# Expert stage: weight slots and token halves placed at other remainders of 128 bytes

## The chip, the cores and the metric

One core of a Trainium2 chip runs the whole program in one launch. The metric is the device time of that core in microseconds (us); lower is better. TensorE is called PE below and its weight loads PEld; DVE is VectorE, ACT ScalarE, POOL GpSimd, SP SyncE.

## The reference

The input is 8 sequences of 512 tokens with 256 features. Four blocks of retention and a small feed-forward part (with group and layer norms) come first, then a mixture of 8 experts, on which the change lies:

```python
x = layernorm(x + attn(x, ...))                 # 4 layers
gates = entmax_bisect(x @ Wr + br)              # 8 experts
h = relu(einsum('td,edf->etf', x, W1) + b1)     # 256 -> 1024
y = einsum('etf,efd->etd', h, W2) + b2          # 1024 -> 256
out = layernorm(x + einsum('td,te->td', y, gates))
```

All is float32 at inputs and outputs.

## The kernel before

**Precision.** A float32 product is made of three matmuls. `mm3` (L1569 to L1571) multiplies the high half of the stationary operand by the high and by the low half of the moving operand, then the stationary low half by the moving high half. A "half" here is the part of a value that one fp32r operand carries (high), or what is left (low); `both` and the pairs of lists hand them in. So every product of the expert stage is three matmuls of 128x512, each with a weight load of its own.

**Work of the expert stage.** The sequences are taken in 4 pairs. In each pair the stage runs over 32 quads (an expert and a block of 256 of its hidden features), 128 quads in all. A quad has 7 products from tokens to hidden (`product`) and 8 products from hidden to output (`down`). That is 21 and 24 matmuls, 45 in a quad and 5,760 in all. Seven and not eight products are needed because a Strassen-like scheme works with sums of weight blocks and sums of token blocks.

**Operands of a quad.** The stationary operands are columns of a weight slot `m_w`: 11 blocks of 128 columns, high halves first (`we_hi`), then the low halves (`we_lo`). There are four slots (`RING`), and quad q uses slot q % 4. The moving operands of `product` are `te_hi` and `te_lo`, the token halves, in two copies: copy 0 for pairs 0 and 2 ("even pairs"), copy 1 for pairs 1 and 3. The moving operands of `down` are `hid_hi` and `hid_lo`.

**Who fills the slots.** In pair 0 POOL forms the sums of weights, ACT writes the high halves (L883) and DVE the low halves (L1251), and SP stores each finished slot to DRAM as `prepared`. In pairs 1 to 3 SP loads the slot back: `load_prepared(q)` waits until quad q - 4 has been used up, and is issued three quads ahead of its own.

**Order of the work.** It is written out by hand. For each quad w, PE runs the products of quad w + 1 between the downs of quad w, so that ACT, DVE and POOL have time for bias, relu and the split of the hidden values. All engines are held together by semaphores with fixed counts.

**Memory.** Everything large lies in one arena of SBUF. `line_up` puts its base at a remainder of 64 when divided by 128, and `place(name, shape, at)` puts a tensor at base + `at` in each partition. All offsets `at` of the expert operands, and all steps inside them, are multiples of 128 bytes, so before the change every slot and every token half starts at remainder 64. One pair of tensors of the earlier layers is different: `h_sp`, the moving operand of the retention product, has rows of 258 floats (1032 bytes). Its four row blocks b = 0, 1, 2, 3 therefore start at remainders 64, 72, 80 and 88.

Of the kernel before, what the change touches and what calls it, by code (L numbers as in the profile page):

```python
# [20 lines left out]
F32R = mybir.dt.float32r  # L21
# [4 lines left out]
P = 128  # L26
# [22 lines left out]
def network(nc, x, Wkqv, Wm1, bm1, Wm2, bm2, gn_g, gn_b, Wf1, bf1, Wf2, bf2, ln_g, ln_b,  # L49
# [7 lines left out]
    B, S, D = x.shape  # L57
# [6 lines left out]
    A_, B_ = 0, 1  # L64
# [23 lines left out]
    SPLIT = 11 * P  # L88
# [13 lines left out]
    with ExitStack() as ctx:  # L102
# [52 lines left out]
        KB = 1024  # L155
        HEAD, TAIL_A = 60 * KB + 256, 14 * KB
        RAW, FOLDED, PLAIN = 0, 16 * KB, 28 * KB
        WORK = [48 * KB + s * (HEAD + TAIL_A) for s in range(SLOTS)]
        LAST = [at + HEAD for at in WORK]
        ENDING = LAST[B_] + TAIL_A  # L160
# [4 lines left out]
        def place(name, shape, at, dt=F32):  # L165
            return nc.alloc_sbuf_tensor_at(name, shape, dt, offset=base + at)
# [14 lines left out]
        def halves(name, s, shape, at):  # L181
# [16 lines left out]
        xs, hs = (place(f"m_{n}s", [P, 2, TB, D], RAW + i * 8 * KB) for i, n in enumerate("xh"))  # L198
        margin = hs[:, 0, 0:2, :].rearrange("p k d -> p (k d)").rearrange("p (n a b) -> p n a b", n=NB, a=E)
        slots = [place(f"m_w{n}", [P, 2, SPLIT], at, F32R)  # L200
                 for n, at in enumerate((WORK[A_] + 8 * KB, FOLDED, PLAIN, LAST[A_]))]
        we_raw = place("we_raw", [P, RAWS, 12 * P], WORK[B_])
        acc = [place(f"m_acc{n}", [P, DC, 2 * S], at) for n, at in enumerate((WORK[A_], WORK[B_] + 50 * KB + 256))]
        t_sum = place("t_sum", [P, 4, S], WORK[A_] + 19 * KB)
        te_hi = [place(f"te_hi{n}", [P, 7, S], at, F32R) for n, at in enumerate((WORK[A_] + 27 * KB, WORK[B_] + 36 * KB + 256))]
        te_lo = [place(f"te_lo{n}", [P, 7, S], at, F32R) for n, at in enumerate((WORK[A_] + 41 * KB, LAST[B_]))]
        sum1, sum2 = (place(f"sum{n + 1}", [P, S], WORK[A_] + (55 + 2 * n) * KB) for n in range(2))
        hid_hi = place("hid_hi", [P, 4, S], WORK[B_] + 12 * KB + 256, F32R)
        full = place("full", [P, 4, S], WORK[B_] + 20 * KB + 256)
        hid_lo = place("hid_lo", [P, 4, S], WORK[B_] + 28 * KB + 256, F32R)  # L210
        out_scaled = place("out_scaled", [P, 4, S], PLAIN + 11 * KB)
        gate_bc = [[place(f"gate_bc{n}{t}", [P, S], at) for t, at in enumerate(places)]
                   for n, places in enumerate(((ENDING, ENDING + 2 * KB), (WORK[B_] + 58 * KB + 256, LAST[A_] + 11 * KB)))]

        bias_rows = place("bias_rows", [E * 2 * FP + E * DC, P], ENDING)

# [1696 lines left out]
def build(nc, x, Wkqv, Wm1, bm1, Wm2, bm2, gn_g, gn_b, Wf1, bf1, Wf2, bf2, ln_g, ln_b,  # L1913
          Wr, br, W1, b1, W2, b2, score_floor, out):
    B, S, D = x.shape
    L = Wkqv.shape[0]
    pairs = B // 2
    h_store = nc.dram_tensor("h_store", ((L + 1) * pairs, 2, S, D), F32, kind="Internal").ap()
    folded = nc.dram_tensor("folded", (L, P, 6 * D), F32, kind="Internal").ap()
    quads = Wr.shape[1] * W1.shape[2] // (2 * P)  # L1920
    prepared = nc.dram_tensor("prepared", (quads, P, 22 * P), F32, kind="Internal").ap()
    gate_rows = nc.dram_tensor("gate_rows", (pairs, Wr.shape[1] * 2 * S), F32, kind="Internal").ap()
    network(nc, x, Wkqv, Wm1, bm1, Wm2, bm2, gn_g, gn_b, Wf1, bf1, Wf2, bf2, ln_g, ln_b,
            Wr, br, W1, b1, W2, b2, score_floor, out, h_store, folded, gate_rows, prepared)
# [23 lines left out]
```

## Time and profile before

| what | us |
|---|---|
| median of 3 runs | 2564.38 (2563.68 to 2564.65) |
| the profiled execution, its own time | 2561.24 |
| span of the profile, first to last instruction | 2559.5 |
| PE busy | 2448.3 |
| DVE busy | 1547.1 |
| ACT busy | 1370.8 |
| POOL busy | 1356.6 |
| mean granted TensorE clock, share of full | 0.987 |

The profile is of one execution. A matmul's busy time overlaps the next one's, since matmuls are pipelined; what a matmul costs is the distance from its start to the next start. The expert stage's first product starts at 1140.7 us and its last down product ends near 2542 us.

### The profile page before, as it was taken

The page shows a single profiled execution, that of the slowest core. Times are in us where ns is not written, and L with a number is a line of the kernel's source. Part 1 is how long each engine was busy: PE and PEld are TensorE (multiplying, and loading weights), DVE is VectorE, ACT ScalarE, POOL GpSimd, SP SyncE. Part 2 cuts the span into 40 slices and gives each one's busy share as a digit, 9 for nine tenths or more (in the row PEclk, how much of TensorE's full clock was granted, in tenths as well). Part 3 has the DMA queues.
Part 4 walks back from the last instruction along what each step waited for, and adds up shares of the span by engine and source line. Part 5 has one row for each costly group of instructions (what it writes and reads, how often), then busy time and mean ns, then how long its engine had stood idle before and what let it go on. Part 6 is the DMA issues. An engine that isn't in the chain of part 4 may idle for free. (4 is left out here: it accounts for less than half of the span.)

```text
span 2559.5 us, 35493 instructions
## 1 busy us (share of the span) xinstructions
PE 2448.3 (96%) x11766; PEld 2033.9 (79%) x11766; DVE 1547.1 (60%) x2976; ACT 1370.8 (54%) x2412; POOL 1356.6 (53%) x1256
## 2 busy tenths in 40 slices
PE   7999999999999999987999999999999999999997
PEld 5788878887888788876878778878888788888886
DVE  1566666656666666677777765656546566455545
ACT  4566666666666666654545554444444444444443
POOL 2244554445444654565777965546555456555454
PEclk9999999999999999998999999999999999999999
DMA  5110111001211112013655564543445344444441
GB/s 161 62 34 33 33 31 62 26 22 33 74 33 33 34 42 67 25 64 134 216 189 179 190 216 169 179 150 144 153 161 186 143 150 147 152 155 171 153 152 70
DMA packets 104582, 283.45 MB, mean 111 GB/s; under 512 B 7024, under 2 KB 77056, under 8 KB 88064
## 3 DMA queue, kind: packets, MB, share of 16 engines
q1 hardware_dynamic: 104320, 281.75, 32.0%
q8 instruction: 69, 1.13, 0.2%
q14 instruction: 65, 0.53, 0.1%
q10 hardware_dynamic: 128, 0.03, 0.0%
HBM read 212.16 MB, written 69.60 MB: 110 GB/s over the span
## 5 line engine op out<-in xcount | busy, mean ns | idle before, releaser
L658 POOL TENSOR_TENSOR hid_lo<-full,hid_hi 128x512 fp32r<-128x512 f32 x384 | 498.6, 1313 | 569.5 <-ACT full L931 460.1
L1365 DVE SCALAR_TENSOR_TENSOR full<-ps,bias_cols,sum 128x512 f32<-128x512 f32 x384 | 288.0, 750 | 207.7 <-PE ps L1571 193.9
L1569 PE MATMUL ps<-hid_hi,m_w 128*128 128x512 f32 x1024 | 403.8, 394 | 0.0
L1570 PE MATMUL ps<-hid_lo,m_w 128*128 128x512 f32 x1024 | 400.7, 391 | 0.0
L1571 PE MATMUL ps<-hid_hi,m_w 128*128 128x512 f32 x1024 | 400.5, 391 | 0.0
L1569 PE MATMUL ps<-te_hi,m_w 128*128 128x512 f32 x896 | 354.5, 396 | 21.0 <-DVE full L1365 14.2
L928 ACT ACTIVATE hid_hi<-ps,bias_cols 128x512 fp32r<-128x512 f32 x128 | 88.3, 690 | 495.9 <-PE ps L1571 495.9
L1570 PE MATMUL ps<-te_lo,m_w 128*128 128x512 f32 x896 | 351.2, 392 | 0.0
L1571 PE MATMUL ps<-te_hi,m_w 128*128 128x512 f32 x896 | 351.0, 392 | 0.0
L935 ACT ACTIVATE hid_hi<-full 128x512 fp32r<-128x512 f32 x256 | 161.7, 631 | 167.3 <-DVE full L1365 167.2
L590 POOL TENSOR_TENSOR pf_sp<-tmp,pf_sp 128x512 fp32r<-128x512 f32 x128 | 163.8, 1317 | 164.8 <-ACT pf_sp L852 164.8
L1569 PEld LDWEIGHTS ps<-hid_hi,m_w 128*128 128x128 f32 x1024 | 193.8, 189 | 40.7 <-issue 0.2
L1571 PEld LDWEIGHTS ps<-hid_hi,m_w 128*128 128x128 f32 x1024 | 193.5, 189 | 40.9
L1570 PEld LDWEIGHTS ps<-hid_lo,m_w 128*128 128x128 f32 x1024 | 193.8, 189 | 38.9
L1569 PEld LDWEIGHTS ps<-te_hi,m_w 128*128 128x128 f32 x896 | 169.5, 189 | 66.9 <-DVE full L1365 19.4
L1352 DVE TENSOR_TENSOR sum<-ps,sum 128x512 f32<-128x512 f32 x128 | 88.4, 691 | 202.5 <-PE ps L1571 181.9
L1571 PEld LDWEIGHTS ps<-te_hi,m_w 128*128 128x128 f32 x896 | 169.7, 189 | 36.1
L1570 PEld LDWEIGHTS ps<-te_lo,m_w 128*128 128x128 f32 x896 | 169.6, 189 | 34.4
L606 POOL TENSOR_SCALAR_AFFINE_SELECT pf_sp<-pf_sp 128x128 fp32r<-128x128 f32 x256 | 65.0, 293 | 196.3 <-DVE pf_sp L1096 196.3
L671 POOL TENSOR_TENSOR m_acc<-m_acc,out_scaled 128x512 f32<-128x512 f32 x124 | 166.7, 1344 | 0.0
L1356 DVE TENSOR_TENSOR sum<-ps,sum 128x512 f32<-128x512 f32 x128 | 88.1, 688 | 119.7 <-PE ps L1571 119.6
L936 ACT ACTIVATE full<-full 128x512 f32<-128x512 f32 x256 | 159.1, 622 | 0.0
(199 smaller groups left out, 5692.9 us busy)
## 6 DMA issues: line engine op xcount, KB each, us to landing
m_w<-prepared SPq DMA_DIRECT2D x96, 1408.0 KB, 6.0
prepared<-m_w SPq DMA_DIRECT2D x32, 1408.0 KB, 5.8
h_store<-h_out SPq DMA_DIRECT2D x32, 512.0 KB, 3.2
we_raw<-in_L_ffn_W SPq DMA_DIRECT2D x64, 256.0 KB, 6.4
gate_bc<-gate_rows SPq DMA_DIRECT2D x64, 256.0 KB, 6.3
h_in<-h_store SPq DMA_DIRECT2D x24, 512.0 KB, 4.3
h_in<-in_L_attn_x SPq DMA_DIRECT2D x8, 512.0 KB, 5.1
raw<-in_L_attn_Wf SPq DMA_DIRECT2D x8, 512.0 KB, 7.9
```

Source lines behind the costliest of these rows:

```text
L590: nc.gpsimd.tensor_tensor(out=lo, in0=full, in1=f32(hi), op=ALU.subtract).then_inc(done, n)
L658: nc.gpsimd.tensor_tensor(out=hid_lo[:, k, :], in0=full[:, k, :], in1=f32(hid_hi[:, k, :]), op=ALU.subtract).then_inc(hid_ready, 1)
L671: nc.gpsimd.tensor_tensor(out=at, in0=at, in1=out_scaled[:, j, :], op=ALU.add).then_inc(acc_added, 1)
L928: nc.scalar.activation(hid_hi[:, k, :], src, ACT.Relu, bias=bias)
L935: nc.scalar.activation(hid_hi[:, k, :], src, ACT.Relu)
L936: nc.scalar.activation(full[:, k, :], src, ACT.Relu).then_inc(relu_ready, 1)
L1352: nc.vector.tensor_tensor(out=sum2[:, :], in0=bank_b, in1=sum1[:, :], op=ALU.add).then_inc(sums, 1)
L1356: nc.vector.tensor_tensor(out=sum3[:, :], in0=bank_b, in1=sum1[:, :], op=ALU.add).then_inc(sums, 1)
L1365: nc.vector.scalar_tensor_tensor(out=full[:, k, :], in0=src, scalar=b1_col(e, 2 * fp + BLOCK_ROW[k]), in1=other[:, :], op0=ALU.add, op1=AL ...
L1569: nc.tensor.matmul(out, w[0], x[0], start=first, stop=False, skip_group_check=True)
L1570: nc.tensor.matmul(out, w[0], x[1], start=False, stop=False, skip_group_check=True)
L1571: return nc.tensor.matmul(out, w[1], x[0], start=False, stop=last, skip_group_check=True)
```

## The change

It moves tensors in the arena and nothing else. Weight slot 0 stays at remainder 64; slot 1 goes 32 bytes up to 96; slot 2 goes 16 bytes up to 80 (it is written as a view that leaves out the first 4 floats of a tensor that is 4 floats longer); slot 3 goes 96 bytes up to 32. Both token halves of even pairs go 160 bytes up to 96. The halves of odd pairs, and `hid_hi` and `hid_lo`, stay at 64. What lies next to a moved tensor (`t_sum`, `sum1`, `sum2`, `out_scaled` and one `gate_bc`) is pushed up by 128 or 256 bytes, which keeps its remainder.

```diff
         slots = [place(f"m_w{n}", [P, 2, SPLIT], at, F32R)
-                 for n, at in enumerate((WORK[A_] + 8 * KB, FOLDED, PLAIN, LAST[A_]))]
+                 for n, at in enumerate((WORK[A_] + 8 * KB, FOLDED + 32, PLAIN, LAST[A_] + 96))]
+        slots[2] = place("m_w2_shifted", [P, 2 * SPLIT + 4], PLAIN, F32R)[:, 4:].rearrange("p (n c) -> p n c", n=2)
-        t_sum = place("t_sum", [P, 4, S], WORK[A_] + 19 * KB)
-        te_hi = [place(f"te_hi{n}", [P, 7, S], at, F32R) for n, at in enumerate((WORK[A_] + 27 * KB, WORK[B_] + 36 * KB + 256))]
-        te_lo = [place(f"te_lo{n}", [P, 7, S], at, F32R) for n, at in enumerate((WORK[A_] + 41 * KB, LAST[B_]))]
-        sum1, sum2 = (place(f"sum{n + 1}", [P, S], WORK[A_] + (55 + 2 * n) * KB) for n in range(2))
+        t_sum = place("t_sum", [P, 4, S], WORK[A_] + 19 * KB + 128)
+        te_hi = [place(f"te_hi{n}", [P, 7, S], at, F32R) for n, at in enumerate((WORK[A_] + 27 * KB + 160, WORK[B_] + 36 * KB + 256))]
+        te_lo = [place(f"te_lo{n}", [P, 7, S], at, F32R) for n, at in enumerate((WORK[A_] + 41 * KB + 160, LAST[B_]))]
+        sum1, sum2 = (place(f"sum{n + 1}", [P, S], WORK[A_] + (55 + 2 * n) * KB + 256) for n in range(2))
-        out_scaled = place("out_scaled", [P, 4, S], PLAIN + 11 * KB)
+        out_scaled = place("out_scaled", [P, 4, S], PLAIN + 11 * KB + 128)
-                   for n, places in enumerate(((ENDING, ENDING + 2 * KB), (WORK[B_] + 58 * KB + 256, LAST[A_] + 11 * KB)))]
+                   for n, places in enumerate(((ENDING, ENDING + 2 * KB), (WORK[B_] + 58 * KB + 256, LAST[A_] + 11 * KB + 128)))]
```

No engine gets an instruction more or less, and none stands at another place in its order.

## Rows read from the trace of the kernel before

**Rows 1.** The page: span, and busy us (share) xinstructions of each engine

```profile
span 2559.5 us, 35493 instructions
PE 2448.3 (96%) x11766; PEld 2033.9 (79%) x11766; DVE 1547.1 (60%) x2976; ACT 1370.8 (54%) x2412; POOL 1356.6 (53%) x1256
```

**Rows 2.** Busy us by stretch, pairs 1 to 3; columns in the first line

```profile
core 0: us, PE busy (x) PEld busy (x) DVE busy (x) ACT busy (x) POOL busy (x), PEclk, DMA share, GB/s
1526.60:1867.30 340.70, 336.83 (x1506) 277.84 (x1505) 198.74 (x308) 153.43 (x273) 180.78 (x141) 0.99 0.44 158
1867.30:2208.00 340.70, 336.86 (x1506) 277.77 (x1505) 198.72 (x308) 153.41 (x273) 180.74 (x141) 0.99 0.45 158
2208.00:2544.00 336.00, 335.10 (x1486) 276.47 (x1485) 171.70 (x257) 149.03 (x262) 168.65 (x133) 1.00 0.41 145
```

**Rows 3.** Waits of PE: who waited, for whom, total us, times, longest us

```profile
PE ps L1569 <- DVE ry_sp L1096: 19.9, 21, 4.3
PE ps L1569 <- DVE full L1365: 14.2, 9, 3.3
```

**Rows 4.** PE's timeline, pair 2: start us, length us, engine, line, operation

```profile
1899.95 0.39 PE L1569 MATMUL ps<-hid_hi,m_w 128*128 128x512 f32 x1
1900.17 0.39 PE L1570 MATMUL ps<-hid_lo,m_w 128*128 128x512 f32 x1
1900.40 0.39 PE L1571 MATMUL ps<-hid_hi,m_w 128*128 128x512 f32 x1
1900.63 0.39 PE L1569 MATMUL ps<-te_hi,m_w 128*128 128x512 f32 x1
...
1901.31 0.39 PE L1569 MATMUL ps<-hid_hi,m_w 128*128 128x512 f32 x1
```

**Rows 5.** Groups by form, weight loads: busy us, mean ns | idle before

```profile
L1570 PEld LDWEIGHTS ps<-hid_lo,m_w 128*128 128x128 f32 x1024 | 193.8, 189 | 38.9
L1570 PEld LDWEIGHTS ps<-te_lo,m_w 128*128 128x128 f32 x896 | 169.6, 189 | 34.4
```

**Rows 6.** PE's timeline, one retention product: its last four row blocks

```profile
393.25 0.28 PE L1569 MATMUL ps<-h_sp,pf_sp 128*128 128x258 f32 x1
...
393.61 0.28 PE L1569 MATMUL ps<-h_sp,pf_sp 128*128 128x258 f32 x1
...
393.97 0.28 PE L1569 MATMUL ps<-h_sp,pf_sp 128*128 128x258 f32 x1
...
394.33 0.28 PE L1569 MATMUL ps<-h_sp,pf_sp 128*128 128x258 f32 x1
394.45 0.28 PE L1570 MATMUL ps<-h_sp,pf_sp 128*128 128x258 f32 x1
394.57 0.28 PE L1571 MATMUL ps<-h_sp,pf_sp 128*128 128x258 f32 x1
```

**Rows 7.** Groups by form, POOL and ACT: splits of 128x1024, and slots written

```profile
L590 POOL TENSOR_TENSOR h_sp<-h_in,h_sp 128x1024 fp32r<-128x1024 f32 x32 | 75.5, 2358 | 52.0 <-ACT h_sp L809 52.0
L590 POOL TENSOR_TENSOR w_plain<-raw,w_plain 128x1024 fp32r<-128x1024 f32 x8 | 19.1, 2390 | 0.0
L809 ACT ACTIVATE h_sp<-h_in 128x1024 fp32r<-128x1024 f32 x32 | 33.6, 1051 | 0.0
L790 ACT ACTIVATE w_plain<-raw 128x1024 fp32r<-128x1024 f32 x8 | 8.3, 1051 | 4.0 <-PE ps L1571 4.0
L1251 DVE TENSOR_TENSOR m_w<-we_raw,m_w 128x1408 fp32r<-128x1408 f32 x32 | 65.5, 2046 | 0.0
```

**Rows 8.** DMA issues: xcount, KB each, median us from issue to landing

```profile
m_w<-prepared SPq DMA_DIRECT2D x96, 1408.0 KB, 6.0
prepared<-m_w SPq DMA_DIRECT2D x32, 1408.0 KB, 5.8
```

**Rows 9.** Timelines: SP issues quad 72's load; PE starts its first product

```profile
1930.13 0.32 SPq L457 DMA_DIRECT2D m_w<-prepared  x1
...
1950.83 0.39 PE L1569 MATMUL ps<-te_hi,m_w 128*128 128x512 f32 x1
```

## The prediction

> **What bounds the kernel now.** I read the page first. PE is busy for 96% of the span, no other engine for more than 60% [rows 1]. Then the expert stage by stretches, because the change lies there alone. A pair takes 340.70 us and PE is busy for 336.8 of it, DVE for 199, POOL for 181, ACT for 153 [rows 2]. Then PE's waits: over the whole program the longest group that lies in the expert stage is 14.2 us behind DVE's L1365 [rows 3]. So PE sets the end, and nothing counts that does not change the distance between its matmuls, or make it wait.
>
> The timeline gives that distance. Six matmuls start between 1899.95 and 1901.31, so a matmul of 512 columns costs 1.36 / 6 = 0.227 us, the same with hidden values as with tokens [rows 4]. At the full clock of 2.4 GHz 512 columns are 213 ns; about 13 ns are left over in each. A quad of 45 matmuls is 45 x 0.2267 = 10.2 us, and 32 quads are 326.4 of the 340.7 us of a pair. The weight load of a matmul has 189 ns on its own track, less than 227 [rows 5]: it runs beside the matmul before.
>
> **The change, part by part.** The order of all engines stays, so every term is a duration that could change.
>
> *1. Matmuls with an operand that moved.* Slots 1 to 3 serve 3/4 of the 5,760 matmuls, 4,320. Slot 0 with the tokens of even pairs adds 64 / 4 = 16 quads x 21 = 336. Together 4,656 matmuls read something at a new remainder. The trace of before has no stationary operand that starts anywhere but at 64, and nothing that starts at 96 or 32. The nearest rows are those of `h_sp`, the moving operand whose row blocks start at 64, 72, 80 and 88. The four triples of one product start at 393.25, 393.61, 393.97 and 394.33, so the triples at 64, 72 and 80 take 0.36 us each; at 88 the first two matmuls take 0.24, as do two thirds of 0.36 [rows 6]. The rows have steps of 0.01 us, so a triple could hide 0.01 us, 3.3 ns in a matmul. The bounds are thus 0 and 3.3 ns x 4,656 = +15.4 us. A gain of the same size can't be excluded by these rows either: -15.4 us. I take 0.3 ns, near nothing, because 72, 80 and 88 read like 64: +1.4 us.
>
> *2. Weight loads.* The same loads begin at 96, 80 and 32. Each may take 227 - 189 = 38 ns more, a fifth of its length, before its track is full [rows 4, 5]. The cover is the matmul before it. If it were gone, each ns over these 38 would cost 4,320 ns, 4.3 us. The nearest row for a start off the usual remainder is again that of rows 6, with no price seen. I take 0.
>
> *3. ACT, DVE and POOL on the moved tensors.* In pair 0 ACT and DVE write 32 slots, 24 of them moved; ACT and POOL write the token halves of even pairs. Rows 7 compare a split of 1,024 elements into `h_sp` (three of four row blocks off remainder 64) with one of 1,024 into `w_plain` at 64: POOL 2358 against 2390 ns, ACT 1051 against 1051. No price, or a gain of 1%. DVE has no such pair; the bounds by POOL's rows are -1% and +1% of 24 x 2046 ns, -0.5 and +0.5 us [rows 7], and it is covered: PE's waits behind DVE in this stage come from L1365 and sum to 14.2 us [rows 3]. I take 0.
>
> *4. DMAs.* A load of a slot lands 6.0 us after its issue, and a store 5.8 [rows 8]. Quad 72's load is issued at 1930.13 and its first product starts at 1950.83, 20.7 us later [rows 9]; so 14.7 us are spare. Loads come once in a quad, about 10.65 us (340.7 / 32) apart [rows 2]. The cost of a misaligned start is bounded by 0 (no row of another remainder) and by the landing itself doubled, +6 us. Even doubled it lands 8.7 us early and before the next is issued (12.0 against 10.65 only just overlaps). The cover is the ring of four slots. Cost 0. In pair 0 a store twice as slow would delay `high_weights`, four quads (over 40 us) later: 0 too.
>
> *5. Neighbours.* They move by whole multiples of 128 bytes: 0.
>
> Sum: +1.4 us on the profiled execution's own 2561.24, hence 2562.6 there. The median of the runs, 2564.38, is 3.1 us above that execution; with the same +1.4 it becomes **2565.8 us**.
>
> Here is a rule against rows: 13 ns above 512 columns stand in each matmul [rows 4]. The Trainium skill (TensorE: Matmul & The Clock Gate, back-to-back measurements in Part 1) gives N / 2.4 + 2.5 ns, 215.7 for 512 columns, so by it 11 ns of ours come from something else. Its Part 2 says that PE has two independent read ports, one for the stream and one for weight loads; by that the 11 ns are no collision of the two reads, and placing them apart returns nothing.
>
> **The rivals.** A difference of 0.2%, 5.1 us, is about what a measurement of this kernel can tell from none.
>
> *Rival A, slower: a stream that starts off a 64-byte boundary takes one piece more.* 2,048 bytes at remainder 64 or 0 are 32 pieces of 64 bytes; at 96 they are 33. A matmul's stream would grow by 1/32 of 213 ns, 6.7 ns. It hits the tokens of even pairs, 64 quads x 21 = 1,344 matmuls: +9 us, **2573 us**. It decides from 3.8 ns on (5.1 us / 1,344). For it: no row shows a start at 96. Against it: `h_sp` at 72, 80 and 88 also starts off such a boundary and takes 0.36 us like 64 [rows 6], though 258 columns there are 16.1 pieces, and 17 are touched either way. That exception makes the row weak, so the rival keeps weight. If the weight loads pay as well, one piece on 8 is 189 / 8 = 24 ns, under the 38 ns of cover. Were the cover not real (PE swaps its weights only after the load has drained), then 4,320 loads would bring up to 24 ns x 4,320 = 104 us.
>
> The Trainium skill (SBUF — State Buffer, Door 1) says that SBUF has lines of 16 bytes, and that each access which crosses to a new line pays. All new remainders are multiples of 16; by it the number of lines stays at 128 for a stream, and rival A does not exist.
>
> *Rival B, faster: the 13 ns are the load's and the stream's reads meeting, and unlike remainders part them.* After the change moving and stationary remainders differ in 4,320 matmuls (all but slot 0 in downs, 768, slot 0 in odd pairs, 336, slot 1 in even pairs, 336). All 13 ns gone: -56 us, **2508 us**. For it: the 13 ns have no cause in the trace. Against it: in rows 6 the stationary `pf_sp` lies at 64 and `h_sp` at 64, then 72, then 80; unlike remainders take the same 0.36.
>
> *Rival C, much slower: the same meeting, but made worse.* Another 13 ns on 4,320 matmuls: +56 us, **2620 us**. Against it the same rows.
>
> *Rival D, nothing at all,* by granted clock alone: clock 0.99 against 1.00 in rows 2 is up to 3.4 us for a pair. This is inside the forecast's own range.
>
> **How the numbers follow.** No change beyond 0.2% (the forecast and D): 0.60. Rival A with its streams alone, 0.19, or with part of the weight loads' cost, 0.08: slower. Rival C 0.04. An unnamed small price that passes 5.1 us (1.1 ns x 4,656, inside the bound of term 1) 0.03. That gives slower 0.34. Rival B, whole or in part, 0.06: faster. The forecast's own range is 2561 (a pair's clock a little better, -3.4) to 2569.5. The range reaches on to A with its full bound: 2564.4 + 15.4 = 2580, and a little of A with weight loads, to 2588. It leaves out B and C and most of the weight-load case, under 2 in 10 together. Low end 2561.
>
> **What would show it.** Right: in the changed kernel six matmuls take 1.36 us in every slot and in both kinds of pair; a pair stays at 340.7 us; weight loads stay at 189 ns; loads of slots land at about 6 us. Slot 2 has a name of its own and so rows of its own; if they differ from the other slots', the 16 bytes matter. Rival A: pairs 0 and 2 grow by 4.5 us each while pair 1 stays. If weight loads pay, pairs 1 and 2 both grow, and the distance follows the slot with a period of four quads. Rival B or C: slot 0 keeps 0.227 us in odd pairs, and the others go to 0.214 or 0.240. I am wrong if any pair's length moves by more than 3 us.

## The result, and the profile after

| | before | changed |
|---|---|---|
| median us | 2564.52 (2563.68 to 2565.03, 4 runs) | 2587.53 (2581.75 to 2591.84, 4 runs) |
| the profiled execution, its own time | 2561.24 | 2581.75 |
| its span | 2559.5 | 2580.0 |

The changed kernel is slower: 1.009 of the time before, 95% interval 1.0078 to 1.0103, 23 us by the medians. The page shows where: PE alone.

```profile
span 2580.0 us, 35493 instructions
PE 2470.9 (96%) x11766; PEld 2030.4 (79%) x11766; DVE 1551.7 (60%) x2976; ACT 1370.8 (53%) x2412; POOL 1355.6 (53%) x1256
```

Against [rows 1] PE is busy 22.6 us longer with as many matmuls; ACT has what it had, POOL 1.0 us less, and DVE 4.6 us more, of which 2.9 us are one group, the split of hidden values (853 ns each before, 876 now). PE does not wait longer for DVE: the 14.2 us of [rows 3] read 12.9 now. The stretches of pairs 1 to 3 answer to [rows 2]. Each is cut where its first token product starts; pair 3 ends with PE's last transposes, about 5 us behind its last down product:

```profile
1524.50:1873.40 348.90, 345.35 (x1507) 279.12 (x1506) 199.33 (x308) 153.48 (x273) 180.17 (x140) 0.99 0.44 154
1873.40:2220.80 347.40, 343.65 (x1507) 277.77 (x1506) 199.52 (x308) 153.41 (x273) 180.31 (x140) 1.00 0.44 155
2220.80:2567.90 347.10, 344.57 (x1497) 278.06 (x1495) 176.09 (x264) 148.95 (x262) 167.88 (x132) 1.00 0.39 140
```

Pairs 1 and 2 took 340.70 us each in [rows 2]. Pair 3, cut the same way in the kernel before:

```profile
2208.00:2547.30 339.30, 336.71 (x1497) 277.66 (x1495) 174.93 (x264) 149.03 (x262) 168.65 (x133) 1.00 0.40 144
```

So the pairs grow by 8.2, 6.7 and 7.8 us, each with all of it in PE's busy time. 7.8 us on 32 x 45 = 1,440 matmuls is 5.4 ns in each. Pair 0 goes only from 385.9 to 387.8 us. PE is idle for some 29 us of it in both kernels, and its granted clock was 0.97 in this execution against 0.96, which gives back up to 3.9 us (0.01 x 386). Averaged over all matmuls of pair 0 that follow one another at the full clock, the distance went from 227.4 to 231.7 ns, 6.2 us on 1,440. The clock records have 27.9 us of the pair at 1.2 GHz before and 21.3 in the changed kernel; half of the difference, 3.3 us, came back. That leaves 2.9 us, and 1.9 were measured:

```profile
1136.70:1524.50 387.80, 358.88 (x1526) 284.42 (x1525) 280.57 (x379) 197.87 (x315) 280.69 (x238) 0.97 0.55 186
```

```profile
1140.70:1526.60 385.90, 356.43 (x1525) 287.34 (x1524) 278.83 (x379) 197.86 (x315) 279.94 (x238) 0.96 0.55 187
```

The first of these two rows is of the changed kernel, the second of the kernel before. The four pairs make 24.6 us. The earlier layers, which the change does not touch, ended 4.0 us sooner in this execution, which leaves the 20.5 us by which the spans differ. Most of the 4.0 is the granted clock: the clock records ahead of the stage have 20.5 us at 1.2 GHz before and 13.7 here, and half of the difference is 3.4 us. This execution is also the fastest of the four of the changed kernel, so the 20.5 us are less than the 23 of the medians.

PE's timeline in pair 2, where [rows 4] had 1.36 us for six matmuls:

```profile
1958.53 0.40 PE L1570 MATMUL ps<-te_hi,m_w 128*128 128x512 f32 x1
1958.77 0.40 PE L1571 MATMUL ps<-te_lo,m_w 128*128 128x512 f32 x1
1959.01 0.39 PE L1572 MATMUL ps<-te_hi,m_w 128*128 128x512 f32 x1
1959.24 0.39 PE L1570 MATMUL ps<-hid_hi,m_w 128*128 128x512 f32 x1
1959.47 0.39 PE L1571 MATMUL ps<-hid_lo,m_w 128*128 128x512 f32 x1
1959.70 0.39 PE L1572 MATMUL ps<-hid_hi,m_w 128*128 128x512 f32 x1
1959.93 0.39 PE L1570 MATMUL ps<-te_hi,m_w 128*128 128x512 f32 x1
```

Six matmuls now take 1.40 us, 233 ns each, and the distances are uneven: 0.24, 0.24, 0.23, 0.23, 0.23, 0.23. No wait stands between them. The rest stayed. Loads of a slot land as in [rows 8], also for slot 2, which is 16 bytes off and has a name of its own; DVE writes that slot in 1952 ns and the others in 2067, [rows 7] had 2046:

```profile
m_w<-prepared SPq DMA_DIRECT2D x72, 1408.0 KB, 6.0
...
m_w_shifted<-prepared SPq DMA_DIRECT2D x24, 1408.0 KB, 6.0
```

```profile
L1252 DVE TENSOR_TENSOR m_w<-we_raw,m_w 128x1408 fp32r<-128x1408 f32 x24 | 49.6, 2067 | 0.0
L1252 DVE TENSOR_TENSOR m_w_shifted<-we_raw,m_w_shifted 128x1408 fp32r<-128x1408 f32 x8 | 15.6, 1952 | 0.0
```

### The profile page after: what moved, and what is told of

Read it like the earlier page. It is cut to its first block and busy times, and to the rows that moved or that the text cites. A ratio compares the mean times of both kernels' runs of the same rounds, so it can differ in the third digit from the quotient of the medians.

```text
span 2580.0 us, 35493 instructions
## 1 busy us (share of the span) xinstructions
PE 2470.9 (96%) x11766; PEld 2030.4 (79%) x11766; DVE 1551.7 (60%) x2976; ACT 1370.8 (53%) x2412; POOL 1355.6 (53%) x1256
## 5 line engine op out<-in xcount | busy, mean ns | idle before, releaser
L1570 PE MATMUL ps<-hid_hi,m_w 128*128 128x512 f32 x768 | 305.1, 397 | 0.0
L1571 PE MATMUL ps<-hid_lo,m_w 128*128 128x512 f32 x768 | 304.9, 397 | 0.0
L1572 PE MATMUL ps<-hid_hi,m_w 128*128 128x512 f32 x768 | 303.0, 395 | 0.0
L1570 PE MATMUL ps<-te_hi,m_w 128*128 128x512 f32 x672 | 268.7, 400 | 18.5 <-DVE full L1366 12.6
L1571 PE MATMUL ps<-te_lo,m_w 128*128 128x512 f32 x672 | 265.8, 396 | 0.0
L1572 PE MATMUL ps<-te_hi,m_w 128*128 128x512 f32 x672 | 265.3, 395 | 0.0
L1570 PEld LDWEIGHTS ps<-hid_hi,m_w 128*128 128x128 f32 x768 | 145.2, 189 | 34.5 <-issue 0.3
L1570 PEld LDWEIGHTS ps<-te_hi,m_w 128*128 128x128 f32 x672 | 127.1, 189 | 57.5 <-DVE full L1366 17.1
L1572 PEld LDWEIGHTS ps<-hid_hi,m_w 128*128 128x128 f32 x768 | 145.1, 189 | 33.5
L1571 PEld LDWEIGHTS ps<-hid_lo,m_w 128*128 128x128 f32 x768 | 145.1, 189 | 32.6
L1572 PEld LDWEIGHTS ps<-te_hi,m_w 128*128 128x128 f32 x672 | 126.8, 189 | 29.9
L1571 PEld LDWEIGHTS ps<-te_lo,m_w 128*128 128x128 f32 x672 | 126.9, 189 | 27.9
```

The costliest lines, as they stand in the source:

```text
L1570: nc.tensor.matmul(out, w[0], x[0], start=first, stop=False, skip_group_check=True)
L1571: nc.tensor.matmul(out, w[0], x[1], start=False, stop=False, skip_group_check=True)
L1572: return nc.tensor.matmul(out, w[1], x[0], start=False, stop=last, skip_group_check=True)
```

## The experiments

Three theories stood at the start. "Off 64": an operand that starts at another remainder than 64 costs something by itself. "Unlike": a stream and the weight load that runs beside it cost something when their remainders differ. "Mixing": what costs is that remainders change from one matmul to the next.

In all that follows pair 3 is the meter. Its granted clock reads 1.00 in every kernel, while pairs 1 and 2 hold from 3.4 to 13.7 us at half clock, which differs from run to run (an average of 0.98 in place of 0.99 is 3.4 us of length). Before, pair 3 took 339.3 us. All the kernels with moved slots or tokens keep the change's pushed neighbours (`t_sum`, `sum1`, `sum2`, `out_scaled`, `gate_bc`), except `arena_96`.

### tokens_only: tokens of even pairs at 96, slots back at 64

```diff
-        te_hi = [place(f"te_hi{n}", [P, 7, S], at, F32R) for n, at in enumerate((WORK[A_] + 27 * KB, WORK[B_] + 36 * KB + 256))]
-        te_lo = [place(f"te_lo{n}", [P, 7, S], at, F32R) for n, at in enumerate((WORK[A_] + 41 * KB, LAST[B_]))]
+        te_hi = [place(f"te_hi{n}", [P, 7, S], at, F32R) for n, at in enumerate((WORK[A_] + 27 * KB + 160, WORK[B_] + 36 * KB + 256))]
+        te_lo = [place(f"te_lo{n}", [P, 7, S], at, F32R) for n, at in enumerate((WORK[A_] + 41 * KB + 160, LAST[B_]))]
```

> Only the token halves of even pairs stand at 96; all weight slots are back at 64. In the changed kernel pairs 1 to 3 each grew by about 8 us (340.7 to 348.9 and 347.4), 5.6 ns in a matmul. Theory 'unlike' (a stream and a weight load that run together at different remainders cost some 5 ns): only the 21 token matmuls of a quad pay, so pair 2 grows by 21/45 of 8 = 3.7 us, pairs 1 and 3 by nothing, in all about +5 us. Theory 'off 64' (only what itself starts off remainder 64 pays): the same, +5 us at most. Theory 'mixing' (remainders that change from matmul to matmul break a steady cadence, whatever they are): pair 2 grows by the full 8 us, hidden-value matmuls at 64 included, pairs 1 and 3 by nothing: about +10 us.

Measured: 2572.86 us against 2564.88, ratio 1.0036 (1.0026 to 1.0047). Pairs 1 to 3:

```profile
1529.00:1870.20 341.20, 337.17 (x1506) 277.65 (x1505) 198.70 (x308) 153.29 (x272) 180.96 (x140) 0.99 0.44 158
1870.20:2218.70 348.50, 344.99 (x1507) 278.76 (x1506) 199.57 (x308) 153.52 (x273) 180.38 (x141) 0.99 0.43 154
2218.70:2558.00 339.30, 336.69 (x1497) 277.57 (x1495) 175.00 (x264) 148.89 (x262) 168.83 (x132) 1.00 0.40 144
```

Pair 2 grows by 7.8 us, twice what the 21 moved matmuls of a quad could bring at 5.6 ns. The 24 matmuls on hidden values, whose stream and load both lie at 64, pay too: averaged over pair 2 at full clock, a matmul on tokens takes 232.6 ns and one on hidden values 231.4, both 227.0 before. "Mixing" had the number.

### slots_only: slots at 64, 96, 80 and 32, tokens back

```diff
-                 for n, at in enumerate((WORK[A_] + 8 * KB, FOLDED, PLAIN, LAST[A_]))]
+                 for n, at in enumerate((WORK[A_] + 8 * KB, FOLDED + 32, PLAIN, LAST[A_] + 96))]
+        slots[2] = place("m_w2_shifted", [P, 2 * SPLIT + 4], PLAIN, F32R)[:, 4:].rearrange("p (n c) -> p n c", n=2)
```

Here and in the kernels that follow up to `one_slot_96`, the tokens of even pairs stand 128 bytes above their old place, since the pushed `t_sum` needs the room. By the count of 128 that is no move. It turned out to be one, so only odd pairs are clean in these runs.

> Only the weight slots stand at 64, 96, 80 and 32; all tokens are back at 64. Theory 'unlike' and theory 'off 64': quads in slots 1 to 3 pay, +6 us in each of pairs 1 to 3, in all about +18 us, and matmuls that read slot 0 keep 227 ns. Theory 'mixing': as the changed kernel, +8 us in each pair, in all about +23 us, and slot 0 pays too, because its matmuls alternate with those of another slot.

Measured: 2589.23 against 2564.88, ratio 1.0093 (1.0072 to 1.0114). Pair 3:

```profile
2229.00:2576.10 347.10, 344.58 (x1497) 278.10 (x1495) 176.17 (x264) 149.04 (x262) 167.92 (x132) 1.00 0.39 140
```

The same 347.1 us as in the changed kernel, whose pair 3 differs in nothing. The slots alone make all of the loss in an odd pair. It is the 8 us of "mixing" and not the 6 of "unlike": slot 0, which was not moved, does not keep 227 ns. Its matmuls take 231.8 ns (tokens) and 230.6 (hidden values) in this pair.

### loads_96: all four slots at 96, all streams at 64

```diff
-                 for n, at in enumerate((WORK[A_] + 8 * KB, FOLDED, PLAIN, LAST[A_]))]
+                 for n, at in enumerate((WORK[A_] + 8 * KB + 32, FOLDED + 32, PLAIN + 32, LAST[A_] + 32))]
```

> All four weight slots stand at 96, all moving operands (tokens and hidden values) at 64: unlike, but the same in every matmul. Theory 'unlike': every matmul pays 5 ns, +8 us a pair, about +28 us in all. Theory 'off 64': the same, since every weight load is off 64. Theory 'mixing': nothing changes from matmul to matmul, so 227 ns and no loss, within 3 us of before.

Measured: 2595.06 against 2564.88, ratio 1.0124 (1.0106 to 1.0141). "Mixing" alone falls: nothing changes from matmul to matmul, and the loss is the largest so far. Pair 3, and PE's timeline in it:

```profile
2232.80:2582.20 349.40, 346.90 (x1497) 278.60 (x1495) 176.93 (x269) 148.88 (x262) 168.20 (x132) 1.00 0.39 140
```

```profile
2299.63 0.40 PE L1571 MATMUL ps<-hid_hi,m_w 128*128 128x512 f32 x1
...
2301.03 0.40 PE L1571 MATMUL ps<-hid_hi,m_w 128*128 128x512 f32 x1
...
2302.43 0.40 PE L1571 MATMUL ps<-hid_hi,m_w 128*128 128x512 f32 x1
```

Twelve matmuls in 2.80 us are 233.3 ns each, 6.6 more than 226.7. Pair 3 is 10.1 us longer, but not all of it is distances. Its last transposes took 1.97 us here and 1.09 before, because the clock fell to half during them (0.84 on average over the last 6.2 us, 1.00 before):

```profile
2580.24 1.97 PE L1793 MATMUL ps<-ident,m_acc 128*128 128x128 f32 x8 [1.68 <-DVE m_acc L1390]
```

```profile
2546.25 1.09 PE L1793 MATMUL ps<-ident,m_acc 128*128 128x128 f32 x8 [1.68 <-DVE m_acc L1390]
```

The first row is of `loads_96`, the second of the kernel before. The other 9.2 us on 1,440 matmuls are 6.4 ns. In the same way 0.7 to 0.9 us of pair 3 in `loads_0`, `loads_32` and `loads_80`, and 0.4 in `loads_128`, are its last transposes. The weight load itself is no longer, 189 ns as in [rows 5]:

```profile
L1570 PEld LDWEIGHTS ps<-te_lo,m_w 128*128 128x128 f32 x896 | 169.8, 189 | 38.8
```

### arena_96: everything in the arena 32 bytes up

```diff
-        line_up()
+        gap = (96 - nc.sbuf_base) % 128
+        if gap:
+            sb("arena_gap", [P, gap], mybir.dt.uint8)
         base = nc.sbuf_base
```

> The whole arena is moved by 32 bytes, so every expert operand, and those of the earlier layers, starts at 96 in place of 64: all like each other, none at 64. Theory 'off 64': every matmul pays, at least +28 us in the expert stage and some in the earlier layers. Theories 'unlike' and 'mixing': no loss, within 3 us of before (only the identity of transposes and small tables stay at 64).

Measured: 2567.88 against 2564.88, ratio 1.0012 (1.0000 to 1.0024). "Off 64" falls: nothing lies at 64, and pair 3 takes 339.4 us.

```profile
1525.30:1870.60 345.30, 341.43 (x1507) 281.31 (x1506) 198.76 (x308) 153.50 (x273) 180.82 (x141) 0.98 0.44 156
...
2215.60:2555.00 339.40, 336.81 (x1497) 277.68 (x1495) 175.03 (x264) 149.10 (x262) 168.60 (x133) 1.00 0.40 144
```

Pairs 1 and 2 of this execution are 4.6 and 4.3 us longer than before, at a granted clock of 0.98 against 0.99: more time at 1.2 GHz (13.7 us in each by the clock records, 3.4 before), not longer distances at 2.4 (227.1 ns on average, 227.0 before).

### Other distances: loads_0, loads_32, loads_80

For slots at 0 every slot goes 64 bytes up, for slots at 32 it goes 96 bytes up:

```diff
-                 for n, at in enumerate((WORK[A_] + 8 * KB, FOLDED, PLAIN, LAST[A_]))]
+                 for n, at in enumerate((WORK[A_] + 8 * KB + 64, FOLDED + 64, PLAIN + 64, LAST[A_] + 64))]
```

```diff
-                 for n, at in enumerate((WORK[A_] + 8 * KB, FOLDED, PLAIN, LAST[A_]))]
+                 for n, at in enumerate((WORK[A_] + 8 * KB + 96, FOLDED + 96, PLAIN + 96, LAST[A_] + 96))]
```

For slots at 80 each slot is a view that begins 4 floats into a longer tensor:

```diff
-        slots = [place(f"m_w{n}", [P, 2, SPLIT], at, F32R)
+        slots = [place(f"m_w{n}", [P, 2 * SPLIT + 4], at, F32R)[:, 4:].rearrange("p (n c) -> p n c", n=2)
```

> All weight slots at 0, all moving operands at 64: a distance of 64 bytes. With slots at 96 (distance 32) every matmul went from 226.7 to 233.3 ns. Theory 'unlike, in 128' (the distance between load and stream counts modulo 128): about as much, +25 to +32 us, perhaps more at the largest distance. Rival 'unlike, in 64' (it counts modulo 64, so 64 is no distance): 226.7 ns and no loss, within 3 us of before. Rival 'some distance is better than none': under 226.7 ns, each ns less is 5.8 us.

> All weight slots at 32, moving operands at 64: the stream lies 32 bytes above the load where before it lay 32 below. If only the size of the distance counts: as with slots at 96, 233.3 ns, +30 us. If the direction counts, or the distance modulo 128 (32 against 96), another value; nothing to say which.

> All weight slots at 80, moving operands at 64: a distance of 16 bytes. Theory 'any unlikeness' (an equal remainder locks the cadence, any other breaks it): 231 to 234 ns, +25 to +32 us. Rival 'a distance under 32 is free', which the retention products suggest (their streams at 72, 80 and 88 took 0.36 us a triple like 64): 227 to 228 ns, under +6 us.

| kernel | slots above streams, odd pairs | median us, ratio (interval) | pair 3, us |
|---|---|---|---|
| loads_80 | 16 | 2588.40, 1.0093 (1.0069 to 1.0118) | 342.6 |
| loads_96 | 32 | 2595.06, 1.0124 (1.0106 to 1.0141) | 349.4 |
| loads_0 | 64 | 2587.05, 1.0086 (1.0062 to 1.0111) | 349.4 |
| loads_32 | 96 | 2600.13, 1.0131 (1.0109 to 1.0153) | 350.8 |

Two of the rows of pair 3, `loads_0` and then `loads_32`:

```profile
2224.50:2573.90 349.40, 346.87 (x1497) 278.56 (x1495) 176.89 (x269) 149.11 (x262) 168.01 (x132) 1.00 0.39 140
```

```profile
2236.60:2587.40 350.80, 348.31 (x1497) 279.58 (x1495) 176.98 (x269) 148.96 (x262) 168.15 (x132) 1.00 0.39 139
```

No distance is free and none is better than 0, so the rivals "in 64" and "some distance is better" fall. The averages at full clock in pair 3 are 233.3 ns at 32 and at 64 bytes and 234.3 at 96, so the price is nearly the same and not in step with the distance. `loads_0` is cheaper by its medians because its even pairs are: pair 2 took 346.1 us there, with tokens 128 and loads 64 bytes up. That was the first sign that 128 bytes are not nothing. The 342.6 us of `loads_80` fit neither of its two cases and have a story of their own, told at the end.

### one_slot_96: slot 1 alone at 96

> Only slot 1 at 96, all else at 64. One load in four is unlike. If each matmul pays for its own load alone: 6.6 ns x 1,440 = +9.5 us. If like triples that alternate with unlike ones pay as well (as the hidden-value matmuls of even pairs did with the tokens at 96): steps in which slot 1 serves either product, two in four, pay in full, +4 us a pair, about +14 us, and the other two steps of four keep 226.7 ns and 10.20 us. If one unlike slot unlocks the cadence for good: +23 us, all four steps long.

```diff
-                 for n, at in enumerate((WORK[A_] + 8 * KB, FOLDED, PLAIN, LAST[A_]))]
+                 for n, at in enumerate((WORK[A_] + 8 * KB, FOLDED + 32, PLAIN, LAST[A_]))]
```

Measured: 2583.48 against 2566.36, ratio 1.0064 (1.0043 to 1.0085); pair 3 takes 343.0 us, +3.7. One load in four at the 6.6 ns of `loads_96` would be 360 x 6.6 = 2.4 us. The middle case of the three holds for odd pairs; the rest of the 17 us lies in the even ones (pair 2: 349.1 us), whose tokens stand 128 bytes off. The timeline shows the cadence coming back. The last matmul that uses slot 1 is the one before 2301.05:

```profile
2299.66 0.40 PE L1569 MATMUL ps<-te_hi,m_w 128*128 128x512 f32 x1
...
2301.05 0.39 PE L1569 MATMUL ps<-te_hi,m_w 128*128 128x512 f32 x1
...
2302.44 0.39 PE L1569 MATMUL ps<-te_hi,m_w 128*128 128x512 f32 x1
...
2303.80 0.39 PE L1569 MATMUL ps<-te_hi,m_w 128*128 128x512 f32 x1
```

Six matmuls take 1.39 us where triples with slot 1 alternate with others, 1.39 again in the first six without it, then 1.36. Operands that are alike pay for some six matmuls after unlike ones; a triple of three is too short to win back the cadence, as I call the steady 226.7 ns. That is what "mixing" had seen: what costs is an unlike pair of operands, with an after-effect on the alike ones that follow.

### tokens_128, tokens_256 and loads_128: is the count 128?

```diff
-        te_hi = [place(f"te_hi{n}", [P, 7, S], at, F32R) for n, at in enumerate((WORK[A_] + 27 * KB, WORK[B_] + 36 * KB + 256))]
-        te_lo = [place(f"te_lo{n}", [P, 7, S], at, F32R) for n, at in enumerate((WORK[A_] + 41 * KB, LAST[B_]))]
+        te_hi = [place(f"te_hi{n}", [P, 7, S], at, F32R) for n, at in enumerate((WORK[A_] + 27 * KB + 128, WORK[B_] + 36 * KB + 256))]
+        te_lo = [place(f"te_lo{n}", [P, 7, S], at, F32R) for n, at in enumerate((WORK[A_] + 41 * KB + 128, LAST[B_]))]
```

`tokens_256` has 256 in both places of the added lines. `loads_128` has that too, and its slots are

```diff
-                 for n, at in enumerate((WORK[A_] + 8 * KB, FOLDED, PLAIN, LAST[A_]))]
+                 for n, at in enumerate((WORK[A_] + 8 * KB + 128, FOLDED + 128, PLAIN + 128, LAST[A_] + 128))]
```

> Only the token halves of even pairs are moved, by 128 bytes: their remainder of 128 is 64 as before, their remainder of 256 is another. In the kernels with moved slots the even pairs, whose tokens also stood 128 bytes up there, took 231 to 234 ns where nothing else was unlike. Theory 'unlike, in 256': pair 2 grows by 7 to 9 us, from 340.7 to about 348, hidden-value matmuls included, pairs 1 and 3 stay; +7 to +12 us in all. Rival 'unlike, in 128' (as the change counts): nothing, 340.7 us in pair 2.

> The token halves of even pairs are moved by 256 bytes, all else as in the run with 128. Theory 'unlike, in 256': no distance, so 226.7 ns and 340.7 us in pair 2, within 3 us of before in all. Rival (any other place than before costs, whatever the remainder, or the period is 512 bytes): pair 2 at about 348 us, as with 128.

> All weight slots are moved by 128 bytes, tokens and hidden values stay at remainders equal in 256: every load stands 128 bytes from every stream. Theory 'unlike, in 256': every matmul pays, 231 to 235 ns, +25 to +35 us, as with distances of 32, 64 and 96. Rival 'unlike, in 128': 226.7 ns and no loss.

| kernel | median us, ratio (interval) | pair 2, us | pair 3, us |
|---|---|---|---|
| tokens_128 | 2576.25, 1.0050 (1.0034 to 1.0066) | 348.7 | 339.3 |
| tokens_256 | 2566.08, 1.0005 (0.9994 to 1.0015) | 341.2 | 339.3 |
| loads_128 | 2590.87, 1.0106 (1.0086 to 1.0125) | 350.1 | 348.7 |

The rows of `tokens_128`, then of `tokens_256`, pair 2:

```profile
1874.40:2223.10 348.70, 345.13 (x1507) 278.67 (x1506) 199.51 (x308) 153.52 (x273) 180.34 (x140) 0.99 0.43 154
```

```profile
1866.30:2207.50 341.20, 337.19 (x1506) 277.95 (x1506) 198.78 (x308) 153.42 (x273) 180.92 (x141) 0.99 0.44 158
```

The row of `loads_128`, pair 3:

```profile
2227.60:2576.30 348.70, 346.20 (x1497) 278.19 (x1495) 176.68 (x267) 149.03 (x262) 168.42 (x132) 1.00 0.39 140
```

A move by 128 bytes leaves the remainder of 128 alone and costs 8.0 us in pair 2; after a move by 256 the pair takes 341.2 us, as an untouched pair can (pair 1 of `tokens_only`). Pair 1 of `tokens_128` took 345.0 us against its expectation, at a clock of 0.98: 13.7 us of it ran at half clock, and its distances at full clock are 227.0 ns as before. The count is 256 bytes. A count of 512 is excluded too: the tokens of `tokens_256` lie 256 bytes off in it, and slot 3 did so before the change, both at full speed. In the kernel before, all expert operands are equal in 256 and not only in 128.

## Why the prediction was right and wrong

The range of 2561 to 2588 held 2587.53, at its very end, and that was luck: it reached so far only for a part of rival A's weight-load case, a mechanism that the runs refute. The case called likeliest, no change, was wrong: the kernel is 0.9% slower. "Slower" had 0.34.

*What bounds the kernel: right.* PE sets the end, and the whole loss is a longer distance between its matmuls: 22.6 us of PE's busy time against 20.5 us of span.

*Term 1: wrong, in the price and in the set.* It took 0.3 ns, with a bound of 3.3 ns, on the 4,656 matmuls that read something moved. Measured are 5.4 ns in pair 3 on all 1,440, also on those where nothing was moved: in `tokens_only` the hidden-value matmuls pay though stream and load both lie at 64. The step that failed is the choice of `h_sp` as the nearest row [rows 6]. It was the nearest by name, a start at 72, 80 and 88, but it is a stream of 258 columns, not 512. Its low half also begins 4,224 bytes above the high half, 128 more than a multiple of 256, so by the count of 256 even the triple that I read as the one at 64 holds unlike operands. All four triples were of the same mixed kind, and their equality said nothing of the case where all is alike.

The partner that I missed stands in the trace of the kernel before. The score product multiplies `hT_sp` and `tu_sp`, alike in 256, and has triples of 256 columns:

```profile
388.57 0.28 PE L1569 MATMUL ps<-tu_sp,hT_sp 128*128 128x256 f32 x1
...
388.93 0.28 PE L1569 MATMUL ps<-tu_sp,hT_sp 128*128 128x256 f32 x1
```

0.36 us for a triple, as in [rows 6]. So at some 256 columns unlike operands show no price (at most the 3.3 ns that the steps of 0.01 us can hide), and at 512 columns they cost up to 7.4 in pair 3. What failed is carrying a price from a short stream to a long one. The rows show one difference between them: the load's 189 ns are longer than the 120 ns from matmul to matmul there, and shorter than the 227 here. Whether that decides was not tested.

*Term 2: right as a duration, wrong in what it concludes for the cost.* The weight load keeps its 189 ns, and 38 ns of room are left; still the distance grows by up to 7.4 ns (`loads_32`, pair 3: 234.3 against 226.8 on average). The price is not in the load's own length. A load that is covered by a stream can still go with a slower stream, by where the two begin.

*Terms 3, 4 and 5: right in their price, nothing.* The writes of slots keep their durations (DVE 65.2 us in all against 65.5), slots land in 6.0 us, and the pushed neighbours cost nothing (339.3 us in pair 3 of `tokens_256`, which has them). One reading in term 4 was wrong: a landing doubled to 12.0 us would come after the next issue, 10.65 us on, not before it. Nothing hung on it.

*Rival A* (a start off 64 bytes takes a piece more) had the sign and not the mechanism: it wanted pairs 0 and 2 long and pair 1 unchanged, and pair 1 grew the most. `arena_96`, where all streams start at 96 in pair 3's 339.4 us, refutes it. *Rivals B and C* named what counts, the relation of load and stream. B had the sign wrong: being alike is the fast case. C had the sign right, but asked 13 ns of 4,320 matmuls and wanted slot 0 spared in odd pairs; it was given 0.04. The sign to look for, "slot 0 keeps 0.227 us in odd pairs", did not show, because it alternates with unlike slots.

*The page on two read ports.* The Trainium skill (TensorE: Matmul & The Clock Gate, Part 2) says that loading the next weights takes no read bandwidth from the running matmul. The runs disagree in part: with the two operands 32 bytes apart the distance from matmul to matmul is 233 ns, with none it is 226.7, with the same instructions. Whatever the ports are, the pace depends on where the two operands lie to each other. The remaining 13 ns above 512 columns never went away at any distance tried, so what they are stays open.

What I did not settle is the mechanism below this. That a collision in the memory is the cause is argued only; no view shows a port or a bank. Nor do the runs tell whether a stream must be like its own weights or like those that are loaded beside it for the next matmul, since the kernels that move all slots move both.

## What to carry to other kernels

When PE is the bound and each matmul of 512 columns has a weight load of its own beside it, put stationary and moving operands at equal remainders of 256 bytes; the remainder itself does not matter (64 and 96 ran alike), the equality does, and it was worth 0.9 to 1.3% here where all or most of the loads stood apart. At 256 columns no price was seen. A push of 128 bytes "to keep the alignment" can be what breaks it, and one unlike buffer slows its neighbours in the order too. Judge an operand's place by the distance between starts of matmuls in steady stretches, not by the length of the load or the matmul.

## What was not expected of the hardware

The price is not a sum over addresses but a cadence that holds or does not. In `loads_80`, with slots 16 bytes above the streams, pair 1 took 346.3 us, and the first part of pair 3 ran at 233.3 ns a matmul. Its four executions also lie furthest apart (2582.81 to 2594.74 us), and the profiled one is the fastest. In pair 3 PE waited once, 0.16 us for DVE, and from there to the end it ran at 226.7 ns at the same addresses. A break alone does not do it: four times before in that pair transposes stood between two matmuls, 0.58 us from the start of the one to the start of the other but without a wait, and 233.3 ns went on. The timeline of that kernel around the pause:

```profile
2326.18 0.40 PE L1571 MATMUL ps<-hid_hi,m_w 128*128 128x512 f32 x1
...
2327.59 0.40 PE L1571 MATMUL ps<-hid_hi,m_w 128*128 128x512 f32 x1
...
2328.48 0.39 PE L1570 MATMUL ps<-te_lo,m_w 128*128 128x512 f32 x1
...
2329.84 0.39 PE L1570 MATMUL ps<-te_lo,m_w 128*128 128x512 f32 x1
```

```profile
2399.65 0.39 PE L1569 MATMUL ps<-te_hi,m_w 128*128 128x512 f32 x1
...
2402.37 0.39 PE L1569 MATMUL ps<-hid_hi,m_w 128*128 128x512 f32 x1
```

Six matmuls in 1.41 us ahead of the pause, six in 1.36 behind it, and twelve in 2.72 us a good while later. Pair 1 shows the way back, from the short cadence to the long one, again at a break:

```profile
1698.82 0.39 PE L1571 MATMUL ps<-hid_hi,m_w 128*128 128x512 f32 x1
...
1700.18 0.39 PE L1571 MATMUL ps<-hid_hi,m_w 128*128 128x512 f32 x1
1700.41 0.60 PE L1765 MATMUL ps<-ident,m_xs 128*128 128x128 f32 x4
...
1701.08 0.39 PE L1570 MATMUL ps<-hid_lo,m_w 128*128 128x512 f32 x1
...
1702.48 0.39 PE L1570 MATMUL ps<-hid_lo,m_w 128*128 128x512 f32 x1
```

Six in 1.36 us ahead of the transposes, six in 1.40 behind them. So at 16 bytes both cadences exist, and a break can switch between them either way; what decides is open. At 0 the short one comes back by itself after some six matmuls (`one_slot_96`); at 32, 64, 96 and 128 it was not seen to hold in pair 3.
